# Prelude of a gated cross-attention block in a new order: sequences 4 to 7 normalised beside the first Q jobs

## What is computed

```python
x = x + tanh(g_xattn[0]) * attention(layernorm(x), ctx, ctx, mask, Wq, Wk, Wv, Wo)
x = x + tanh(g_ffn[0]) * ffn(layernorm(x), ...)

def layernorm(x, eps=1e-05):
    m = mean(x, axis=-1); v = var(x, axis=-1)
    return (x - m) / sqrt(v + eps)

# attention: q, k, v = query @ Wq, key @ Wk, value @ Wv; q, k rotated
logits = 30.0 * tanh(q @ k * 0.0884 / 30.0)
weights = softmax(where(mask, logits, -1e30)); out = (weights @ v) @ Wo
```

## Time and profile before

| | |
|---|---|
| timed runs | 788.84, 789.41, 790.84 us; median 789.41 |
| profiled execution | 787.43 us, its span 785.6 us |
| busy, of the span | PE 733.1 us (93%), DVE 609.8 (78%), POOL 504.6 (64%), ACT 428.7 (55%) |
| DMA | 41.53 MB, mean 53 GB/s |
| mean granted clock of TensorE | 0.973 |

### The profile page before, as it was taken

One profiled execution on the slowest core, in us unless ns is written; L12 is line 12 of the kernel. 1 busy time (PEld: TensorE's weight loads), 2 busy tenths in 40 slices (PEclk: granted clock), 3 DMA queues, 4 the chain that ended last, 5 costly groups with the idle time before them and its releaser, 6 DMA issues. The chain is left out here.

```text
span 785.6 us, 11042 instructions
## 1 busy us (share of the span) xinstructions
PE 733.1 (93%) x3394; PEld 605.7 (77%) x3394; DVE 609.8 (78%) x930; ACT 428.7 (55%) x772; POOL 504.6 (64%) x377
## 2 busy tenths in 40 slices
PE   3768999999999999999999999999778689999998
PEld 3657788888888888888888888888656568888786
DVE  6658979879797887979889887988877588788521
ACT  4446666656565665565666656665453344555520
POOL 5428677776677777757786775776686456656400
PEclk9989999999999999999999999999898799999999
DMA  9500102200200210030020002002220234442011
GB/s 275 149 13 15 42 16 66 67 1 14 94 15 28 92 30 0 15 104 5 27 99 23 1 28 95 0 1 65 64 64 0 53 88 98 103 108 46 1 68 40
DMA packets 70621, 41.53 MB, mean 53 GB/s; under 512 B 23242, under 2 KB 63050, under 8 KB 70570
## 3 DMA queue, kind: packets, MB, share of 16 engines
q1 hardware_dynamic: 70570, 40.90, 18.6%
HBM read 38.77 MB, written 2.11 MB: 52 GB/s over the span
## 5 line engine op out<-in xcount | busy, mean ns | idle before, releaser
L567 POOL TENSOR_TENSOR aT_lo<-attn,aT_hi 128x512 fp32r<-128x512 f32 x64 | 83.1, 1299 | 96.0 <-ACT aT_hi L758 96.0
L501 POOL TENSOR_TENSOR q_sin<-q_sin,q_tab 128x512 f32<-128x512 f32 x64 | 82.7, 1293 | 41.4 <-ACT q_sin L659 38.7
L55 PE MATMUL ps_o<-wo_hi,aT_hi 128*128 128x512 f32 x256 | 102.6, 401 | 4.7 <-POOL acc L573 3.5
L55 PE MATMUL bank_q<-xT_hi,wq_hi 128*128 128x512 f32 x256 | 101.1, 395 | 3.2 <-issue 3.2
L57 PE MATMUL ps_o<-wo_hi,aT_lo 128*128 128x512 f32 x256 | 101.8, 398 | 0.0
L56 PE MATMUL ps_o<-wo_lo,aT_hi 128*128 128x512 f32 x256 | 101.5, 396 | 0.0
L56 PE MATMUL bank_q<-xT_lo,wq_hi 128*128 128x512 f32 x256 | 100.6, 393 | 0.0
L57 PE MATMUL bank_q<-xT_hi,wq_lo 128*128 128x512 f32 x256 | 100.4, 392 | 0.0
L666 ACT CAST qT_hi<-bank_q 128x512 fp32r<-128x512 f32 x64 | 37.5, 587 | 114.4 <-DVE bank_q L912 114.4
L493 POOL TENSOR_TENSOR probs<-probs,keepT 128x512 f32<-128x512 f32 x64 | 83.1, 1298 | 13.5 <-ACT probs L768 13.4
L904 DVE TENSOR_TENSOR bank_q<-bank_q,q_tab 128x512 f32<-128x512 f32 x64 | 44.7, 699 | 45.2 <-ACT q_sin L659 45.0
(11 more groups left out here) (214 smaller groups left out, 2074.5 us busy)
## 6 DMA issues: line engine op xcount, KB each, us to landing
wq_raw<-in_Wq SPq DMA_DIRECT2D x32, 256.0 KB, 2.8
wo_raw<-in_Wo SPq DMA_DIRECT2D x8, 1024.0 KB, 5.3
packed<-in_gate_q SPq DMA_DIRECT2D x40, 64.0 KB, 2.2
packed<-in_up_q SPq DMA_DIRECT2D x40, 64.0 KB, 2.2
packed<-in_down_q SPq DMA_DIRECT2D x10, 256.0 KB, 3.4
acc<-in_x SPq DMA_DIRECT2D x8, 256.0 KB, 5.3
cT_raw<-in_ctx SPq DMA_DIRECT2D x8, 256.0 KB, 5.7
wk_raw<-in_Wk SPq DMA_DIRECT2D x8, 256.0 KB, 2.6
```

The source lines that it names most:

```text
L55: nc.tensor.matmul(out, w_hi, m_hi, start=first, stop=False)
L501: nc.gpsimd.tensor_tensor(by_seq(q_sin[:]), by_seq(q_sin[:]), q_tab[:, 1, :].unsqueeze(1).to_broadcast([P, HALF, T]), ALU.mult).then_inc(q ...
L567: nc.gpsimd.tensor_tensor(aT_lo[:], attn[:], aT_hi[:].bitcast(F32), ALU.subtract).then_inc(a_split, 1)
```

## The change

- The normalisation runs in four parts of two sequences instead of 2, 2 and 4. `xn` has four buffers instead of two (it now reaches into the raw half of the second Wo buffer, and SP's `load_wo(1)` waits until the eighth transposition is done).
- Sequences 4 and 5 are normalised by DVE right behind the moments and `cos_q(0)`; sequences 6 and 7 by ACT in two passes each: `centre_x` adds minus the mean, `scale_x` multiplies by the inverse deviation.
- PE: `prep(4)` ahead of `make_k(0)`, `prep(5)` and V job 3 behind it, then `make_q(2)`, `prep(6)`, `prep(7)`, `make_q(3)`. V job 3 stood in slot 0, V job 4 in slot 1; they are now in the prelude and in slot 0. By the same table the V jobs of sequences 2, 3, 4 of each later pair stand at 16 p - 2, 16 p - 1, 16 p instead of 16 p - 1, 16 p, 16 p + 1.
- Context sequences 4 and 5 are prepared in the prelude, 6 and 7 in slot 0 (before: 4 and 5 in slot 0, 6 and 7 in slot 1).
- `live_rows` is made by ACT, `keep` by POOL, `fold` by POOL (a memset and four affine_selects), all three formerly by DVE.

The diff, cut to its core:

```diff
-V_AT = (-5, -4, -1, 0, 1, 3, 5, 7)
-NORM_PARTS = (slice(0, 2), slice(2, HALF), slice(HALF, B))
+V_AT = (-5, -4, -2, -1, 0, 3, 5, 7)
+NORM_PARTS = (slice(0, 2), slice(2, 4), slice(4, 6), slice(6, 8))
...
-        xn = over("xn", [P, 2, C], F32, wo_at[1] + 4096)
+        xn = over("xn", [P, HALF, C], F32, wo_at[1] + 4096)
...
+                sp.wait_ge(x_T, B)
                 load_wo(1)
...
+                nc.gpsimd.memset(fold[:], 0.0).then_inc(fold_done, 1)
+                for j in range(4):
+                    pool.wait_ge(fold_done, j + 1)
+                    nc.gpsimd.affine_select(out=fold[:].rearrange("p (i c) -> p i c", i=4), in_=fold[:].rearrange("p (i c) -> p i c", i=4),
+                                            compare_op=ALU.not_equal, fill=1.0, base=-32 * j, pattern=[[0, 4], [-1, 32]],
+                                            channel_multiplier=1).then_inc(fold_done, 1)
...
                 ctx_rest(1)
+                pool.wait_ge(mask_step, 4)
+                nc.gpsimd.tensor_scalar(keep[:], mask_f[:], dead[:], None, ALU.max).then_inc(keep_done, 1)
+                split_w("wq", 0, 1)
                 split_w("wk", 0, 0)
-                split_w("wq", 0, 1)
+                invert_std(2)
                 ctx_rest(3)
                 sin_q(0)
-                invert_std(2)
+                invert_std(3)
                 split_w("wq", 0, 2)
...
+                def centre_x(b):
+
+                    act.wait_ge(mean_done, 1)
+                    act.wait_ge(x_T, b - HALF + 1)
+                    nc.scalar.activation(xn[:, b % HALF, :], acc[:, b, :], ACT.Identity,
+                                         bias=minus_mean[:, b, :]).then_inc(x_centred, 1)
+
+                def scale_x(b):
+
+                    act.wait_ge(rstd_done, 4)
+                    act.wait_ge(x_centred, b - HALF - 1)
+                    nc.scalar.activation(xn[:, b % HALF, :], xn[:, b % HALF, :], ACT.Copy,
+                                         scale=rstd[:, b, :]).then_inc(xn_late, 1)
...
-                    if s < 2:
-                        prep_ctx(HALF + 2 * s)
-                        prep_ctx(HALF + 2 * s + 1)
+                    if s == 0:
+                        prep_ctx(6)
+                        prep_ctx(7)
...
+                def norm_mean():
+
+                    bs = NORM_PARTS[3]
+                    nc.vector.tensor_scalar(minus_mean[:, bs, :], moments[:, bs, 0:1], -1.0, None, ALU.mult).then_inc(mean_done, 1)
...
                 make_v(2)
                 make_q(1)
+                prep(4)
                 make_k(0)
-                prep(4)
                 prep(5)
+                make_v(3)
                 make_q(2)
                 prep(6)
                 prep(7)
```

More of the change, by code:

```diff
@@ L695, in _ @@
                 round_w("wq", 0, 0)
+                act.wait_ge(mask_step, 3)
+                nc.scalar.copy(live_rows[:], live[:].to_broadcast([P, T])).then_inc(rows_done, 1)
                 prep_x(2)
                 prep_x(3)
+                round_w("wq", 0, 1)
+                prep_ctx(2)
                 round_w("wk", 0, 0)
-                prep_ctx(2)
-                round_w("wq", 0, 1)
+                prep_ctx(3)
                 round_v(1)
-                prep_ctx(3)
                 turn_q(0)
+                centre_x(6)
+                round_v(2)
                 round_w("wq", 0, 2)
-                round_v(2)
+                scale_x(6)
+                centre_x(7)
                 round_q(0)
                 turn_q(1)
+                prep_x(4)
+                scale_x(7)
+                round_w("wq", 0, 3)
+                prep_x(5)
                 turn_k(0)
-                round_w("wq", 0, 3)
                 round_q(1)
+                round_v(3)
+                turn_q(2)
                 round_k(0)
-                turn_q(2)
-                prep_x(4)
-                prep_x(5)
+                prep_x(6)
+                prep_x(7)
                 act.wait_ge(ld_gates, 32)
@@ L718, in _ @@
                 turn_q(3)
-                prep_x(6)
-                prep_x(7)
+                prep_ctx(4)
+                prep_ctx(5)
                 round_q(3)
@@ L975, in _ @@
                 v_rest(1)
-                for b in range(HALF, B):
-                    norm_moments(b)
+                norm_moments(4)
+                norm_moments(5)
                 norm_var(2)
+                norm_moments(6)
+                norm_moments(7)
+                norm_apply(4)
+                norm_var(3)
+                norm_mean()
                 dve.wait_ge(keep_T, 1)
@@ L985, in _ @@
                 cos_q(0)
+                norm_apply(5)
                 v_rest(2)
                 add_q(0)
-                norm_apply(4)
                 cos_q(1)
                 q_rest(0)
+                x_rest(4)
                 cos_k(0)
                 add_q(1)
+                x_rest(5)
                 add_k(0)
-                norm_apply(5)
                 q_rest(1)
+                v_rest(3)
                 cos_q(2)
                 k_rest(0)
-                x_rest(4)
-                x_rest(5)
+                x_rest(6)
                 add_q(2)
-                norm_apply(6)
-                norm_apply(7)
+                x_rest(7)
                 q_rest(2)
                 cos_q(3)
-                x_rest(6)
-                x_rest(7)
+                ctx_rest(4)
+                ctx_rest(5)
                 add_q(3)
-                dve.wait_ge(id_done, 1)
-                nc.vector.reduce_sum(r_tot[:, 0:32], ident[:].rearrange("p (i c) -> p c i", i=4), AX_X).then_inc(fold_done, 1)
-                dve.wait_ge(fold_done, 1)
-                nc.vector.tensor_copy(fold[:].rearrange("p (i c) -> p i c", i=4),
-                                      r_tot[:, 0:32].unsqueeze(1).to_broadcast([P, 4, 32])).then_inc(fold_done, 1)
                 q_rest(3)
```

29 lines of the change are left out of this document (16 added, 13 removed).

## The result

| | kernel before | changed kernel |
|---|---|---|
| timed runs, median (lowest to highest) | 789.12 us (787.88 to 790.84) | 778.68 us (777.84 to 779.50) |
| ratio, 95% interval | | 0.9861 (0.9841 to 0.9880) |
| span of the profiled execution | 785.6 us | 776.2 us |

The changed kernel is faster by 1.4%, 11 us by the ratio (9.5 to 12.5) and 10.4 us by the medians. 9.0 us were forecast, 780.4 us; the range was 776.6 to 784.0. A second set of timed runs of the changed kernel gave 779.79 us, a ratio of 0.9875 (0.9841 to 0.9908).

A forecast was written before the change was run, and what follows sets the result against it. Bound by chains of dependent steps in the prelude (TensorE idle 11.75 us), then by TensorE itself; 9.0 up to weigh(0) + 0.85 (a) - 0.85 (b) = 9.0 us, 789.4 - 9.0 = 780.4 us, range 776.6 to 784.0.

The forecast's parts named there:

- Steps 1 to 7: Prelude from turn_q(0) to weigh(0), followed operation by operation: weigh(0) at 54.05 instead of 63.07, 9.0 us earlier.
- step 6: Prelude, turn_q(3) to round_q(3): two ctx_rest beside sin_q(3) end at 43.3; round_q(3) at 43.95, 8.6 us earlier.
- step 2: ACT in the prelude: scale_x(6) waits for invert_std(3) until 27.0; turn_q(1), queued behind it, runs 28.7 to 29.9.
- step 7: ACT's list from round_q(3) to the first tanh stays the same, 4.2 us; tanh at 48.15, 9.0 us earlier.
- (a): Slot 1, without ctx 6, 7 and a V job: normalise(0) about 1.3 us sooner; gain 0 to 1.2, taken 0.85.
- (b): PE's stop before weigh(0) grows to 3.9 us, lower clock behind it; loss 0 to 1.7, taken 0.85.
- A: Prelude: rope chains faster, PE not stopped between 26.2 and 44.7, clock stays up; gain some 12 us, 777.4; chance 0.12.
- B: Prelude: an ACT in-order wait 2 to 4 us later, clock falls, (a) fails; gain 3 to 5, 785.4; chance 0.13.
- C: Slots 14, 30 and 46 stop TensorE, 3.8 us in each; slower, about 792; chance 0.02.
- D: No effect: make_q(4) in the prelude is held by something else than sequences 4 to 7; 789.4; chance 0.03.

The follow-up runs named there:

- e3: Changed kernel with sequences 6 and 7 normalised by DVE, one pass each, instead of two ACT passes each; 776.52 us, ratio 0.9824.
- e6: Changed kernel with Wo roundings and context sequences 6 and 7 behind the first tanh and exp on ACT in slot 0; 777.09 us, ratio 0.9845.
- e9: Changed kernel with 14 extra matmuls of 128x512, result unused, in the stop before weigh(0); 779.16 us, ratio 0.9865.
- after_again: The changed kernel, unedited, timed and profiled once more; 779.79 us, ratio 0.9875.
- e1: Changed kernel with V jobs and context sequences put back where they were before, leaving the new normalisation order; 778.55 us, ratio 0.9860.
- e2: Kernel before with only the moves of V jobs and context sequences; 791.86 us, ratio 1.0015.
- e7: Changed kernel with the edits of e3 and e6, V job 4 one slot later, add_q(3) and q_rest(3) ahead of ctx_rest(4); 773.50 us, ratio 0.9818.
- e10: e7 with POOL doing the rests of Wo parts 2 and 3 ahead of a_rest(0) in slot 2; 773.68 us, ratio 0.9788.
- e4: Changed kernel with two xn buffers instead of four and load_wo(1) without its wait; 782.52 us, ratio 0.9909.

## Why the prediction was right

The forecast of 9.0 us stands beside 9.4 in the spans and 10.4 to 11 in the timed runs. Up to weigh(0), 9.0 were forecast and 8.4 measured, and for the reason given: this is the part that the walk got right. The rest of the agreement is luck, as shown below: 0.8 us came from slots 1 to 4, in which two terms, both far too small, nearly cancelled. Point by point, in distance from make_q(0):

| | walk | changed kernel |
|---|---|---|
| turn_q(1) | 9.6 | 9.99 |
| make_q(2) | 12.3 | 12.63 |
| make_q(3) | 17.3 | 17.85 |
| make_q(4) | 21.4 | 22.11 |
| round_q(3) | 24.9 | 25.61 |
| first tanh | 29.1 | 29.76 |
| weigh(0) | 35.0 | 35.61 |

**Steps 1 to 7** hold, each 0.3 to 0.7 us late. What made them late is small and spread: the wait of scale_x(6) ended 0.2 us later in this measure (28.39 - 20.23 = 8.16 against 27.0 - 19.06 = 7.94, since POOL's rstd took 0.88 us and not 0.70), and the passes behind it started 0.63 and 0.61 us apart, where the walk had 0.6. The two ctx_rest of step 6 are no part of it: from the first of them to add_q(3) it took 1.77 us (45.12 - 43.35), where I had 1.75. DVE timeline of the changed kernel, which answers to the earlier trace rows:

```profile
24.60 0.82 DVE L926 TENSOR_SCALAR xn<-acc,moments,rstd 128x512 f32<-128x512 f32 x1
...
26.72 1.08 DVE L926 TENSOR_SCALAR xn<-acc,moments,rstd 128x512 f32<-128x512 f32 x1
...
43.35 1.85 DVE L938 TENSOR_TENSOR cT_lo<-cT_raw,cT_hi 128x512 fp32r<-128x512 f32 x2
45.12 0.68 DVE L952 TENSOR_TENSOR bank_q<-bank_q,q_sin 128x512 f32<-128x512 f32 x1
```

norm_apply(4) and (5) took 0.82 and 1.08 (I had 0.8 and 1.1). The stops came out at 1.34, 1.26, 0.48 and 3.55 where the walk had 1.15, 1.4, 0.6 and 3.9. In e3 and e6 the ACT passes of step 2 and the list of step 7 were taken away one at a time: turn_q(1) came 0.86 us sooner (1.2 in the prediction) and weigh(0) 1.0; for step 7 weigh(0) came 1.7 sooner, as expected of e6.

**Terms (a) and (b)** were put at +0.85 and -0.85, and neither is what happened. The stretch from weigh(0) to weigh(1) took 2.22 us more at the lower clock (9.50 against 7.28), where (b) charged 0.85; and from weigh(1) to weigh(4) the changed kernel took 3.04 us less (24.50 against 27.54), where (a) allowed 0.85. Of these 3.04, DVE's three small operations, which no longer met POOL's, are 2.33 (0.87 against 3.20); this term stands nowhere in the prediction. The premise of (a), that DVE comes to normalise(0) 1.3 us sooner, holds where the clock stays up: in e9 it does so 1.44 us behind weigh(0), before 2.82, and PE does not wait before project(0). That the sum, put at 0, came out at 0.82 (0.72 in after_again) is luck.

**Two readings of the rows were off**, without weight in the sum. Beside the stop before 43.04 DVE worked for 3.59 us, not under 3. And for the lower clock behind 33.22 I counted 1.4 us; the PE timeline, in which that Q job ends its issue at 38.05, gives 4.83 us for 3.2 of work, 1.6.

**The clock rule that I read from the rows was too simple.** I had taken a stop of over 3.2 us as the condition. In the changed kernel the clock was at 0.73 from 13.96 to 20.23, with no stop above 1.14 us in it; in the kernel before it stayed at 1.00 over stops of 1.05 and 1.75. In e1 a stop of 2.58 us was followed by 0.68, in e9 one of 1.87. Behind a stop of 2.49 us in e6 it fell (0.80 up to weigh(1)), behind one of 2.48 in e2 it stayed at 1.00. The length of one stop does not decide it; what does, these runs leave open. The stretches, of the changed kernel, the kernel before and e1:

```profile
13.96:20.23 6.27, 4.27 (x20) 3.66 (x21) 5.24 (x10) 4.19 (x9) 4.62 (x6) 0.73 1.13 332
```
```profile
14.68:19.06 4.38, 2.62 (x21) 2.38 (x21) 4.38 (x9) 2.63 (x5) 4.38 (x4) 1.00 1.10 346
```
```profile
54.26:59.59 5.33, 5.33 (x18) 4.32 (x19) 5.23 (x10) 3.27 (x8) 2.66 (x2) 0.68 0.01 2
```

**The two rules of the Trainium skill.** By the first, an operation which DVE and ACT both can do is faster on DVE where DVE has a performance mode for it ("Perfetto Trace Analysis", Optimizing Scalar/DVE Operations). Against it I had set the row of 1.51 us beside POOL, by which the two ways were equal. e3 sides with the rule: 0.85 us per pass on DVE, beside POOL, against two passes of 0.72 on ACT. The second rule of the Trainium skill, the exclusive hold of the shared pair ("SBUF — State Buffer", Who interferes with whom), agrees with step 6: two ctx_rest beside sin_q took 1.85 us where two with POOL idle took 1.29 (48.08 in the same kernel).

**Rivals.** A (no stop left) did not come; e7 and e10, which remove more of them, are what it looks like. B (less) is half seen in e4: with two buffers the in-order waits on ACT bring weigh(0) 2.2 us later, and about 3 us of the gain are lost. C (K and V in one slot) is excluded by the dense 11.26 us of slot 14; from weigh(4) to weigh(50) both orders take 391.0 to 391.3 us. D is excluded by the result.

The remaining difference to the timed runs (1 to 2 us) has no cause of its own that I can show: starts differ by 2.4 us and rests by 2.7 between executions of kernels that do the same there.

## What to carry to other kernels

In a prologue where no engine is full, walk the in-order queues one by one and look for steps that wait for work of later use. Here three stops of TensorE, 11.75 us, came from normalising and preparing four sequences behind the rope steps of the first jobs. A new order, with the buffers that it needs, gave 8.4 us. An operation moved to a less busy engine is no gain if its new place is in the chain: two passes on ScalarE cost 1 us against leaving them on VectorE in a gap. And look at the durations in the new trace as well as at its waits: DVE's three small operations took 0.87 us or up to 3.98 by what POOL did beside them, so that a step which comes sooner can meet what it missed before.

## What was not expected of the hardware

- The granted clock fell to 0.73 in a stretch of 6.3 us with stops of at most 1.14 us, in the stage in which the loads keep the DMA engines full, and stayed at 1.00 in another kernel's same stage.
- Three DVE operations on 128x192 took 0.87 us together in POOL's pause and up to 3.98 us beside POOL's work.
- Filling a stop of 3.5 us with 14 matmuls kept the clock up there, and it fell behind a later wait, of 1.87 us.
- POOL's tensor_scalar on 128x128 took 0.61 us at 17.62 in the changed kernel, where I had 0.3 to 0.5.
- The start of the first Q job differed by 2.4 us between executions, by the arrival of x and by the clock, more than several of the edits studied here are worth.
